# Two-layer attention, time-mix and expert kernel: projections ahead of turns, late weights and the attention's first inputs moved into the projection phase, and the shared groups of the experts reordered

## The chip, the cores and the metric

The kernel runs on one core of a Trainium2 chip. Its time is the device time of one execution, in microseconds (us). TensorE (PE) multiplies, VectorE (DVE) and ScalarE (ACT) work on rows, GpSimd (POOL) does small arithmetic and issues the indirect transfers, and SyncE (SP) issues nearly all other transfers.

## The reference

Input x is 2 sequences of 2048 tokens, 256 wide (4096 tokens). Two layers follow, each a parallel block: both halves read the same layer norm.

```python
xn = _layernorm(x)
x = x + attention(xn, w_qkv, w_out) + binarized_ffn(xn, w1, b1, w2, b2)
xn = _layernorm(x)
x = x + time_mix(xn, ...) + experts(xn, router, gate, up, down, shared_...)
```

- Attention: 16 heads of 16, rotary tables on q and k, causal softmax over 2048 tokens, projection by w_out.
- Binarized FFN: hidden 1024; each weight matrix is sign(w) times the mean of |w| of its row; gelu.
- Time-mix: x and the token before are blended by time_mix_k, _v and _r; k, v, r are their projections; a stable recurrence (running maximum p, numerator q) runs over the tokens, its result times sigmoid(r) is projected by W_o.
- Experts: softmax over 8 experts, the best 2 kept; silu(x gate) * (x up), then down (width 128); a shared expert of width 256 runs on every token.

## The kernel before, in words

The program is a row of phases. Within a phase every engine has its own program, and they meet on semaphores; between phases all engines meet.

**Projection phase** (`qkv_phase`). The 4096 tokens are 8 groups of 512 (G = 8). For each group: layer-norm statistics on DVE (`scales`, L280 to L290), the root on POOL (`ln.root`, L299 to L316), the normalized rows on ACT (`scaled`, L322), 8 transposes on PE (`ln.turn`, L332), a high part (ACT, L341) and a low part (DVE `low`, L346), and products of three float16 pairs on PE (`heads` for q and k, `values` for v, L102). DVE applies the rotary tables (`products` L741, `rotated` L749 and L750) and takes the low parts (`last`, L755). The stages are software-pipelined: `step(at)` gets the groups that stand at each stage, `rolling` runs the steps, the first and last written out, the middle ones in a hardware loop of two steps (`Fori`). `w.vector` and `w.tensor` (L133 to L180) find one power-of-two scale for w_qkv: the maximum over partitions goes through PE (L153, L155), then DVE writes the scaled high and low parts. SP loads x, weights and rotary tables, stores normalized parts (L662), q and k (L670) and v (L673); in its second step it also issues the loads of the weights that later phases use (`late_weights.load`, L393 to L400).

**Attention phase** (`attention_phase`). 8 iterations, each of one sequence and one group of heads. Softmax needs the row maxima before it; they are computed by entries that run ahead of the exponentials: an entry multiplies k by q on PE (L1253), adds the mask (L1259), and DVE reduces it (L1187); a "turn" entry transposes the maxima (L1245, L1174, L1177) and SP sends them into extra rows of q (`send_m`, L1083). `HEAD` entries run before the first exponential (L1216) of iteration 0, the others between its steps. Before them come the phase's own loads of ident, mask, k and q (L1059, L1045, L1052), and PE and ACT turn the late weights (L425, L438) in 12 groups: 4 ahead of the first entry, 8 between entries.

**Time-mix phase** (`rwkv_phase`). 8 groups of 512 tokens pass five stages; x of a group is loaded by L1776. The router's logits need the normalized parts of all 8 groups (`load_parts`, L1781). DVE then chooses experts and slots (L1871 to L1929), after which POOL scatters the rows to their experts by 64 indirect transfers (L1838). At its start SP clears the semaphores of the first two phases (`retired`).

**Expert phase** (`moe_phase`). `FIRST` shared groups run first, then 46 tiles of 128 rows of one expert each (about 2.6 us a tile), then the other shared groups. `shared(n)` is gate and up (L102 on PE, L2448 on ACT, L2349 and L2354 on DVE), `shared_out(n)` is down (PE) and L2381 (DVE). POOL gathers the experts' results back (64 transfers, L2288), the last 24 after the last tile, and DVE adds them (`finish`, L2406 and L2411).

## Time and profile before

| | |
|---|---|
| three timed runs | 1685.28 us (median), 1674.21, 1686.58 |
| profiled execution | 1673.15 us, span in the trace 1671.4 us |
| busy: PE, DVE, ACT, POOL | 78%, 76%, 59%, 19% of the span |
| mean granted TensorE clock | 0.907 of full speed |
| projections | 0 to 146 us |
| attention, 8 iterations | 146 to about 1012 us |
| time-mix, scatter included | 1231 to 1448 us |
| experts | 1448 us to the end |

The rows further down are of three kinds. A timeline row gives start, duration, engine, source line, operation, output and inputs, count, and in brackets the idle time ahead of it on that engine with what ended it. A DMA row on SPq gives the time that the issuing of its transfers took. A window row gives the busy time of each engine in a stretch, and the granted clock.

### The profile page before, as it was taken

How to read it: one execution, taken by the hardware profiler on the slowest of the kernel's cores; microseconds unless marked ns; L12 is line 12 of the kernel's file. 1: busy time of each engine (PE TensorE's matmuls, PEld its weight loads, DVE VectorE, ACT ScalarE, POOL GpSimd, SP SyncE). 2: the span in 40 equal slices, each digit the busy share in tenths (PEclk: the TensorE clock that was granted, in tenths of full speed). 3: DMA queues.
4: the chain of work that ended last, by engine and by line, in shares of the span. 5: the costliest groups of instructions: out<-in, count | busy, mean ns of one | idle time of the engine just before them, and what ended most of it. 6: DMA issues, size and time to landing. Idle time of an engine off the chain costs nothing. (4 is left out here: it accounts for less than half of the span.)

```text
span 1671.4 us, 27976 instructions
## 1 busy us (share of the span) xinstructions
PE 1300.7 (78%) x9558; PEld 589.5 (35%) x9558; DVE 1271.8 (76%) x1880; ACT 986.5 (59%) x1291; POOL 321.7 (19%) x574
## 2 busy tenths in 40 slices
PE   2783887888888888798888985988736866579987
PEld 1442322222222222222222211666513333258754
DVE  3994788988779788898888922578666999475677
ACT  2442355777768677787787895556335656246642
POOL 2210000110101101011100201322100057500563
PEclk9886589999899999999999998999957897789999
DMA  6787202140321303223031024556543044676865
GB/s 184 250 266 181 52 8 41 20 91 6 74 41 29 83 5 74 41 37 76 6 76 37 12 40 130 159 192 202 173 141 127 25 136 152 201 239 201 251 197 201
DMA packets 159863, 186.27 MB, mean 111 GB/s; under 512 B 19572, under 2 KB 135796, under 8 KB 158708
## 3 DMA queue, kind: packets, MB, share of 16 engines
q1 hardware_dynamic: 153304, 167.65, 35.7%
q0 software_dynamic: 6144, 16.79, 3.1%
q8 instruction: 73, 1.20, 0.3%
q14 instruction: 54, 0.44, 0.1%
q10 hardware_dynamic: 288, 0.20, 0.1%
HBM read 100.94 MB, written 83.36 MB: 110 GB/s over the span
## 5 line engine op out<-in xcount | busy, mean ns | idle before, releaser
L1216 ACT ACTIVATE att_prob<-att_score,late_score_scale 128x1024 f32<-128x1024 f32 (+3 forms) x640 | 594.5, 988 | 214.2 <-PE att_score L1318 212.4
L1187 DVE TENSOR_REDUCE att_m_part<-att_mx 128x2 f32<-128x1024 f32 (+3 forms) x408 | 473.4, 1160 | 98.8 <-PE att_mx L1259 50.4
L1302 PE MATMUL att_pv<-att_prob,att_v 128*32 128x512 f32 (+3 forms) x2560 | 316.4, 568 | 0.5 <-POOL att_prob L1151 0.2
L1318 PE MATMUL att_score<-att_qop,att_kop 50*128 50x512 f16 (+3 forms) x1280 | 257.3, 364 | 9.0 <-ACT att_prob L1216 5.9
L1253 PE MATMUL att_mx<-att_kop,att_qop 48*128 48x512 f16 (+3 forms) x944 | 177.4, 361 | 106.3 <-DVE att_m_part L1187 101.6
L1151 POOL TENSOR_SCALAR_AFFINE_SELECT att_prob<-att_prob 128x256 f32<-128x256 f32 x256 | 102.9, 406 | 762.2 <-ACT att_prob L1216 762.0
L1187 DVE TENSOR_REDUCE att_m_part<-att_mx_one 128x1 f32<-128x384 f32 (+1 forms) x336 | 221.1, 658 | 32.8 <-PE att_mx_one L1253 27.0
L1318 PEld LDWEIGHTS att_score<-att_qop,att_kop 50*128 50x128 f16 x1280 | 69.4, 95 | 281.4 <-ACT att_prob L1216 192.7
L1253 PE MATMUL att_mx_one<-att_kop,att_qop 48*128 48x384 f16 (+1 forms) x336 | 132.4, 394 | 20.3 <-DVE att_m_part L1187 16.7
L2066 PE MATMUL rwkv_prod<-rwkv_xm,late_mixT 128*128 128x512 f32 x192 | 101.2, 682 | 36.9 <-ACT rwkv_kvr L2029 25.1
L1253 PEld LDWEIGHTS att_mx<-att_kop,att_qop 48*128 48x128 f16 x944 | 50.8, 96 | 174.7 <-DVE att_m_part L1187 158.1
L1838 POOL DMA_INDIRECT rows<-rwkv_xs,routing_slot_i x64 | 67.2, 1050 | 141.6 <-DVE routing_slot_i L1929 111.4
L2288 POOL DMA_INDIRECT moe_yg<-results,routing_slot_i x64 | 66.0, 1032 | 128.7 <-DMA results<-moe_y 109.9
L1598 ACT ACTIVATE ffn_gelu<-ffn_hid_ps,late_b,late_a 128x512 f32<-128x512 f32 x64 | 49.2, 778 | 66.9 <-PE ffn_hid_ps L1639 51.3
L1546 DVE SCALAR_TENSOR_TENSOR ffn_hid<-ffn_gelu,late_hid_scale_scale,ffn_hid 128x512 f16<-128x512 f32 x64 | 52.0, 847 | 44.8 <-ACT ffn_hid L1606 44.8
L1302 PEld LDWEIGHTS att_pv<-att_prob,att_v 128*32 128x32 f32 x2560 | 51.4, 110 | 70.9 <-issue 46.4
L2066 PEld LDWEIGHTS rwkv_prod<-rwkv_xm,late_mixT 128*128 128x128 f32 x192 | 41.2, 221 | 89.2 <-issue 76.0
L1639 PE MATMUL ffn_hid_ps<-ffn_xp,late_w1T 128*128 128x512 f16 x256 | 63.7, 386 | 4.7 <-ACT ffn_gelu L1598 4.1
L1657 PE MATMUL ffn_out_ps<-late_w2T,ffn_hid 128*128 128x256 f16 x512 | 63.6, 279 | 0.0
L1253 PEld LDWEIGHTS att_mx_one<-att_kop,att_qop 48*128 48x128 f16 x336 | 32.1, 96 | 82.6 <-DVE att_m_part L1187 71.0
L2012 ACT ACTIVATE rwkv_xm<-rwkv_x,late_unmix 128x512 f32<-128x512 f32 x48 | 30.2, 710 | 51.3 <-DMA rwkv_x<-xn1T 51.3
L1657 PEld LDWEIGHTS ffn_out_ps<-late_w2T,ffn_hid 128*128 128x128 f16 x512 | 51.6, 101 | 11.5 <-issue 0.8
(259 smaller groups left out, 1921.6 us busy)
## 6 DMA issues: line engine op xcount, KB each, us to landing
moe_xt<-rows SPq DMA_DIRECT2D x46, 256.0 KB, 3.5
results<-moe_y SPq DMA_DIRECT2D x46, 256.0 KB, 2.8
qk<-qkv_parts SPq DMA_DIRECT2D x32, 256.0 KB, 3.8
va<-qkv_v SPq DMA_DIRECT2D x8, 1024.0 KB, 6.4
att_v<-va SPq DMA_DIRECT2D x8, 1024.0 KB, 5.2
rows<-att_zeros SPq DMA_DIRECT2D x8, 864.0 KB, 6.2
att_kop<-qk SPq DMA_DIRECT2D x48, 128.0 KB, 4.9
att_qop<-qk SPq DMA_DIRECT2D x186, 32.0 KB, 3.1
```

Source lines behind the costliest of these rows:

```text
L1151: nc.gpsimd.affine_select(out=at, in_=at, compare_op=ALU.is_ge, fill=0.0, base=0, pattern=[[0, 2], [1, P]], channel_multiplier=-1)\
L1187: nc.vector.tensor_reduce(cells[:, sides[0]:sides[-1] + 1, some], bank.rearrange("p a (h w) -> p a h w", w=w), AX.X, ALU.max).then_inc(m_f ...
L1216: nc.scalar.activation(prob[:, r % (PROBS * HP), :, n0:], score[:, r % 2, :, n0:], ACT.Exp, scale=late_weights.score_scale[:, 0:1])\
L1253: op = nc.tensor.matmul(bank[a][:, n * w:(n + 1) * w], qop[rows, slot, t, hp, i * P:(i + 1) * P], kop[rows, slot, hp, c * GT:c * GT + w], ...
L1302: op = nc.tensor.matmul(pv[at, n0:], v[:, slot, j, at], prob[:, (st * HP + h // 2) % (PROBS * HP), h % 2, n0:], start=(j == 0), stop=(j == ...
L1318: op = nc.tensor.matmul(score[:, r % 2, hh, n0:], kop[rows, slot, hp, j * P:(j + 1) * P], qop[rows, slot, t, hp, n0:], start=True, stop=True)
L1546: nc.vector.scalar_tensor_tensor(hid[:, slot, 1, m], gelu[:, m % GELUS], hid_scale.scale[:, 0:1], hid[:, slot, 0, m], ALU.mult, ALU.subtra ...
L1639: op = nc.tensor.matmul(hid_ps[:, m % 2], w1T[:, k, m * P:(m + 1) * P], xp[:, slot, part, k], start=(k == 0 and part == 0), stop=(k == KC ...
L1657: op = nc.tensor.matmul(out_ps[:, j], hid[:, slot, part, m, at], w2T[:, m], start=(m == 0 and part == 0), stop=(m == FC - 1 and part == 1))
L1838: nc.gpsimd.indirect_dma_start(rows_d[part], bass.IndirectOffsetOnAxis(slot_i[:, k, j:j + 1], 0), xs[:, c % XP, i], None)\
L2066: op = nc.tensor.matmul(prod[:, (n * NO + o) % PRODS], wT[:, w, k, c * P:(c + 1) * P], xm[:, b, w, k], start=(k == 0), stop=(k == KC - 1))
L2288: nc.gpsimd.indirect_dma_start(yg[:, at, k], None, results_d[part], bass.IndirectOffsetOnAxis(slot_i[:, k, j:j + 1], 0))\
```

## The change

1. **Projections.** The loops are written out (`unrolled` in place of `rolling`). On PE the weight scale's product stands ahead of the first turn, and in each step `heads` stands ahead of `turn`. The layer-norm statistics get two buffers. Of DVE's work `low` of the new group stands after the rotation of the one before. From the third group on, each step turns one of the 12 groups of late weights, the other 6 follow the last step; their banks are two halves of the bank of v. The late weights' loads are issued one SP step later, with the mask and the lift rows of the attention.
2. **The attention's inputs.** k and the first quarter of q of iteration 0 are loaded after the stores of group 6, ahead of those of group 7; the other three quarters and v after the last step. `HEAD` ends 3 entries after the first turn entry, where it was the second turn entry; the maxima's sends stand ahead of the second iteration's loads.
3. **Time-mix.** x of groups 2 and 3 is loaded ahead of the parts of groups 2 to 7; parts of groups 0 and 1 are loaded again behind these, for the experts. The clearing of semaphores moves to the end of SP's program.
4. **Experts.** `FIRST` goes from 2 to 3. Groups 0 and 1 read the parts left by the time-mix phase. Down weights, expert weights and shared groups are interleaved anew; after the tiles `shared(FIRST)` stands ahead of the last `tile_out`.

```diff
@@ SP, projections
-                if at[1] and not at[2]:
+                if at[2] and not at[3]:
                     late_weights.load(nc, sp, *late_ds)
+                    att_in.load_constants(sp, mask_d, lift_d)
                 if at[2]:
                     store_xn(*at[2])
                 if at[3]:
                     store_heads(*at[3])
-
-            rolling(sp, step, 4)
+                    if at[3][0] == G - 2:
+                        sp.wait_ge(qk_stored[0], 16 * QK * KC * (1 + G // 2))
+                        att_in.load_k(sp, qk_d, 0, 0, 0)
+                        att_in.load_q(sp, qk_d, 0, 0, 0, 0, att_in.first_in[0])
+
+            unrolled(step, 4)
+            for t in range(1, att_in.QB):
+                att_in.load_q(sp, qk_d, 0, 0, 0, t, att_in.second_in if t == 1 else att_in.rest_in[0])
@@ DVE, projections
+                for p in range(QK):
+                    if mid:
+                        products(*mid, p)
+                        rotated(*mid, p)
                 if new:
                     low(*new)
-                if mid:
-                    products(*mid, 0)
-                    rotated(*mid, 0)
-                    products(*mid, 1)
-                    rotated(*mid, 1)
@@ PE, projections
             def step(at):
                 new, mid = at
+                if new and not mid:
+                    w.tensor(nc, pe, qk_ps[0:1, 0, 0, 0:P], qk_ps[:, 0, 0, P:P + 1], ident[:, :], ones[:, :])
+                if mid:
+                    ...
+                    heads(*mid, 0)
+                    if mid[0] >= late_from:
+                        late(mid[0])
+                    heads(*mid, 1)
                 if new:
                     ln.turn(nc, pe, new[0], new[1], ident[:, :])
@@ attention
-    HEAD = ahead.index(("turn", 1)) + 1
+    HEAD = ahead.index(("turn", 0)) + 3
@@ SP, attention
-                load(0, 1, 1)
                 for t in range(LATE - 1):
                     send_m(0, 0, t, False)
+                load(0, 1, 1)
@@ SP, time-mix
-            for signal in retired:
-                sp.sem_clear(signal)
             load_x(0)
             load_x(1)
...
                 if m == B:
-                    for g in range(XP, G):
+                    load_x(B)
+                    load_x(B + 1)
+                    for g in range(XP, G + XP):
                         load_parts(g)
...
             groups(step, 5)
+            for signal in retired:
+                sp.sem_clear(signal)
@@ experts
-    FIRST = 2
+    FIRST = 3
@@ DVE, experts
             shared(0)
-            down_weights(slice(SHARED, SHARED + E))
-            for e in range(E):
+            for e in range(E // 2):
                 weights(e)
             shared(1)
             shared_out(0)
             owners()
+            for e in range(E // 2, E):
+                weights(e)
+            shared(2)
             shared_out(1)
+            dve.wait_ge(down_high, 2)
+            down_weights(slice(SHARED, SHARED + E))
+            shared_out(2)
             tile_x(0)
@@ PE, experts
+            shared(FIRST)
             tile_out(NTILES - 1, before)
-            shared(FIRST)
```

How the instructions stand at three places, before and after. In the start of PE's program, `qkv_qk_ps` is the bank of the products and of the weight scale's transpose, `qkv_turned` that of the turns. Before:

```order
L332 MATMUL qkv_turned<-qkv_ident,qkv_ln_xn 128x128 x8
L153 MATMUL qkv_qk_ps<-qkv_ident,qkv_w_qkv_top 1x128
L155 MATMUL qkv_qk_ps<-qkv_w_qkv_apart,qkv_ones 128x1
L590 UNCONDITIONAL_BRANCH
L590 ISA
L328 REGISTER_ALU
L332 MATMUL qkv_turned<-qkv_ident,qkv_ln_xn 128x128 x8
L833 ISA
L102 MATMUL qkv_qk_ps<-qkv_ln_hi,qkv_w_qkv_hi 128x512
```

After, the same engine from its start:

```order
L153 MATMUL qkv_qk_ps<-early_ident,qkv_w_qkv_top 1x128
L155 MATMUL qkv_qk_ps<-qkv_w_qkv_apart,qkv_ones 128x1
L338 MATMUL qkv_turned<-early_ident,qkv_ln_xn 128x128 x8
L102 MATMUL qkv_qk_ps<-qkv_ln_hi,qkv_w_qkv_hi 128x512
L102 MATMUL qkv_qk_ps<-qkv_ln_hi,qkv_w_qkv_lo 128x512
```

The scale's two products have moved ahead of the first turn, and the first group's products ahead of the second turn. The next place is SP at the end of the projections and the start of the attention. Before:

```order
L670 DMA qk<-qkv_parts 16x16x512 x4
L673 DMA va<-qkv_v 128x4x512
L670 DMA qk<-qkv_parts 16x16x512 x4
L673 DMA va<-qkv_v 128x4x512
L603 UNCONDITIONAL_BRANCH
L1056 UNCONDITIONAL_BRANCH
L1059 DMA att_ident<-in_ident 128x128
L1059 DMA att_mask<-in_mask 128x320
L1045 DMA att_kop<-qk 16x2x2048 x6
L1052 DMA att_qop<-qk 16x2x512 x18
L1064 DMA att_kop<-in_lift 2x8192 x2
L1073 DMA att_v<-va 128x2048
```

After, with the attention's buffers named `early_`:

```order
L744 DMA qk<-qkv_parts 16x16x512 x4
L747 DMA va<-qkv_v 128x4x512
L642 DMA early_kop<-qk 16x2x2048 x6
L649 DMA early_qop<-qk 16x2x512 x6
L744 DMA qk<-qkv_parts 16x16x512 x4
L747 DMA va<-qkv_v 128x4x512
L649 DMA early_qop<-qk 16x2x512 x18
L654 DMA early_v<-va 128x2048
```

Twelve loads stand between the last two groups' stores, and 19 more come ahead of the phase's end. The third place is PE after the last tiles of the experts; `moe_tile_p` is a tile's hidden, `moe_hid_p` a shared group's. Before, the last two tiles' down products and the first shared group behind them:

```order
L102 MATMUL moe_out_ps<-moe_down_p,moe_tile_p 128x256
L102 ISA
L102 MATMUL moe_out_ps<-moe_down_p,moe_tile_p 128x256 x5
L102 ISA
L102 MATMUL moe_out_ps<-moe_down_p,moe_tile_p 128x256
L102 ISA
L102 MATMUL moe_out_ps<-moe_down_p,moe_tile_p 128x256 x5
L102 MATMUL moe_gate_ps<-moe_xp,experts_shared_p 128x512 x6
L102 MATMUL moe_up_ps<-moe_xp,experts_shared_p 128x512 x6
```

After, from the last but one tile's down products:

```order
L102 MATMUL moe_out_ps<-moe_down_p,moe_tile_p 128x256 x5
L102 MATMUL moe_gate_ps<-routing_xp,experts_shared_p 128x512 x6
L102 MATMUL moe_up_ps<-routing_xp,experts_shared_p 128x512 x6
L102 MATMUL moe_gate_ps<-routing_xp,experts_shared_p 128x512 x6
L102 MATMUL moe_up_ps<-routing_xp,experts_shared_p 128x512 x6
L102 ISA
L102 MATMUL moe_out_ps<-moe_down_p,moe_tile_p 128x256
L102 ISA
L102 MATMUL moe_out_ps<-moe_down_p,moe_tile_p 128x256 x5
```

One shared group's gate and up now stand between the last two tiles' down products.

## Rows read from the trace of the kernel before

**Rows 1.** Busy us of PE, PEld, DVE, ACT, POOL, then the clock, by stretch.

```profile
39.60:137.70 98.10, 74.11 (x420) 45.19 (x418) 93.45 (x136) 43.91 (x76) 18.81 (x75) 0.88 0.75 241
156.20:189.30 33.10, 24.95 (x173) 13.06 (x173) 24.83 (x32) 4.69 (x8) 0.00 (x0) 0.50 0.55 124
189.30:200.00 10.70, 9.06 (x40) 1.75 (x39) 8.80 (x12) 5.80 (x8) 2.44 (x6) 0.50 0.01 3
323.00:426.00 103.00, 86.03 (x777) 25.72 (x772) 86.07 (x107) 76.15 (x86) 13.25 (x33) 0.97 0.23 47
```

**Rows 2.** Timelines of DVE and PE, the first 40 us.

```profile
7.56 1.75 DVE L174 TENSOR_REDUCE qkv_w_qkv_top<-qkv_w_qkv_w 128x1 f32<-128x1536 f32 x1
...
16.38 1.94 PE L332 MATMUL qkv_turned<-qkv_ident,qkv_ln_xn 128*128 128x128 f32 x8 [16.38 <-ACT qkv_ln_xn L322]
...
18.88 0.28 DVE L133 TENSOR_REDUCE qkv_w_qkv_top_all<-qkv_qk_ps 1x1 f32<-1x128 f32 x1 [9.56 <-PE qkv_qk_ps L153]
...
23.74 1.40 DVE L280 BATCH_NORM_STATS2 qkv_ln_stats<-qkv_xin 128x6 f32<-128x256 f32 x4
...
26.02 1.23 DVE L346 TENSOR_TENSOR qkv_ln_lo<-qkv_turned,qkv_ln_hi 128x1024 f16<-128x1024 f32 x1
...
39.63 1.23 DVE L741 TENSOR_TENSOR qkv_by_cos<-qkv_qk_ps,qkv_cos 128x1024 f32<-128x1024 f32 x1 [1.97 <-PE qkv_qk_ps L102]
```

**Rows 3.** Timeline of SP, the late weights' loads, first and last.

```profile
4.25 0.43 SPq L393 DMA_DIRECT2D staging_raw<-in_L_attn_W_k  x1
...
17.31 1.79 SPq L400 DMA_DIRECT2D late_first<-in_L_attn_time_first  x1
```

**Rows 4.** Timelines of DVE and SP, last stores to first maximum.

```profile
135.25 2.42 DVE L755 TENSOR_TENSOR qkv_parts<-qkv_rot,qkv_parts 128x1024 f16<-128x1024 f32 x2
...
136.56 2.57 SPq L670 DMA_DIRECT2D qk<-qkv_parts  x4
...
147.15 2.66 SPq L1045 DMA_DIRECT2D att_kop<-qk  x6
...
149.86 8.56 SPq L1052 DMA_DIRECT2D att_qop<-qk  x18
...
157.03 0.69 DVE L1187 TENSOR_REDUCE att_m_part<-att_mx 128x4 f32<-128x512 f32 x1 [10.35 <-PE att_mx L1259]
```

**Rows 5.** DMA part of the page: KB each, median us to landing.

```profile
qk<-qkv_parts SPq DMA_DIRECT2D x32, 256.0 KB, 3.8
```

**Rows 6.** Timelines of SP, ACT, DVE and POOL, time-mix phase to the first scatter.

```profile
1231.24 0.19 POOL L1826 MEMSET experts_ones<- 20x128 f32 x1 [54.09 <-POOLq L1367]
...
1234.52 1.28 SPq L1776 DMA_DIRECT2D rwkv_x<-xn1T  x2
...
1285.27 3.79 ACT L2012 ACTIVATE rwkv_xm<-rwkv_x,late_unmix 128x512 f32<-128x512 f32 x6 [17.17 <-DMA rwkv_x<-xn1T]
...
1286.64 4.07 DVE L1936 SCALAR_TENSOR_TENSOR rwkv_xm<-rwkv_x,late_mix,rwkv_xm 128x512 f32<-128x512 f32 x6 [5.50 <-ACT rwkv_xm L2012]
...
1294.31 0.17 DVE L1944 COPY rwkv_p<-rwkv_p 128x2 f32<-128x2 f32 x1 [3.60 <-ACT rwkv_kvr L2029]
...
1343.17 1.45 POOL L1838 DMA_INDIRECT rows<-rwkv_xs,routing_slot_i  x1 [111.43 <-DVE routing_slot_i L1929]
```

**Rows 7.** Timeline of PE, expert phase: the first tile.

```profile
1482.40 0.88 PE L102 MATMUL moe_gate_ps<-moe_xh,moe_expert_p 128*128 128x256 f16 x6 [1.23 <-DVE moe_xh L2387]
```

**Rows 8.** Timelines of PE and POOL, behind the last tile.

```profile
1610.62 0.84 PE L102 MATMUL moe_out_ps<-moe_down_p,moe_tile_p 128*128 x6 [2.31 <-DVE moe_tile_p L2354]
...
1615.62 0.94 POOL L2288 DMA_INDIRECT moe_yg<-results,routing_slot_i  x1 [7.20 <-DMA results<-moe_y]
...
1649.26 1.08 POOL L2288 DMA_INDIRECT moe_yg<-results,routing_slot_i  x1 [0.30 <-issue]
...
1653.25 2.78 PE L102 MATMUL moe_out_ps<-moe_down_p,moe_hid_p 128*128 128x256 f16 x24
...
1661.43 5.30 PE L102 MATMUL moe_out_ps<-moe_down_p,moe_hid_p 128*128 128x256 f16 x24 [5.40 <-DVE moe_base L2381]
```

312 lines of the change are left out of this document (172 added, 140 removed).

## The prediction

> **What bounds the kernel now.** I read the busy time of each engine by stretch first, and from it which engine each stretch waits for; then the timelines around the five places that the change touches; then the stores' landing time. In the steady projections DVE is busy 93.45 of 98.10 us, PE 74.11 [rows 1]: DVE bounds, with 4.65 us of idle in eight groups. In a later iteration of the attention PE and DVE are both busy 86 of 103 us at a clock of 0.97, and neither loses much to one other engine [rows 1]. The places with real gaps are five: DVE's 9.56 us wait for the weight scale's product at the start [rows 2]; the 19.4 us from the end of the last rotation (135.25 + 2.42 = 137.67) to the first maximum at 157.03 [rows 4]; the 33.1 us of maxima before the first exponential, in which DVE is busy only 24.83 [rows 1]; ACT's 17.17 us wait for x in the time-mix phase [rows 6]; and the end, where PE waits 5.40 us for DVE ahead of its last products [rows 8]. The change goes to all five. What it leaves alone is the bulk: iterations 1 to 7 of the attention, the FFN, the scatter, the 46 tiles.
>
> **Term A, the start of the projections.** The maximum of the weights is reduced by 7.56 + 1.75 = 9.3, but its product stands behind a turn that starts at 16.38, and so DVE gets it at 18.88; from there to the next group's statistics at 23.74 are 4.9 us of scale and split [rows 2]. With the product first, 9.3 + 0.6 + 4.9 gives 14.8, so the weights are no longer last. The turn stays where it was (it waits for ACT), ends at 18.3, and the high part (ACT, about 1) and the low part (1.23 for the second group's at 26.02 [rows 2]) follow: the first group's heads can start at 20.8, no longer behind the second turn. The first of them took 4.6 us at half clock; the rotation starts at 25.4, where it started at 39.63 [rows 2]: 14.2 us earlier, less 1.23 for the second group's low part, which now follows the first rotation: 13.0. What is late next is x of the fourth group. SP spends 17.31 + 1.79 - 4.25 = 14.9 us on the late weights' loads [rows 3]. They now start at about 17.6, behind x and tables of the third group, and end at 32.5; with the store behind them x is issued at 34 and, landing in about 4 as the store's 3.8 [rows 5], is there at 38.3. DVE wants it at 36.2 and loses 2.1. **A = 10.9** (6 to 14).
>
> **Term B, the steady steps.** Between 0 and DVE's whole idle of 4.65 us [rows 1]. PE's work grows by a late turn a step; a turn of 8 blocks takes 1.94 at half clock [rows 2], one of 4 half that, and PE has 24 us to spare in eight groups, so it is hidden; if PE were to be late, six times 1.0 would be the price. The turn's later place on PE is covered by the second statistics buffer. I take **B = 1.5**, nearer to nothing, since most of the idle is spread over short gaps. DVE then ends at T = 137.7 - 12.4 = 125.3.
>
> **Term C, the change-over.** Before, 19.4 us. Now SP bounds it. The stores of group 6 end about 7 us ahead of T and land 3.8 later [rows 5]; then 12 loads: 2.66 for k and a third of 8.56 for q [rows 4], 5.5 together, to T + 2.1; the stores of group 7, 2.57 and 0.65 for v, which could have gone at T - 1, to T + 5.3; the 18 loads of q, 8.56, to T + 13.9, and v. The phase ends there, and as the inputs are in place the first maximum follows in about 1.5: T + 15.4 against T + 19.4. The last six late turns on PE and their copies on ACT (6 times 0.6) lie beside SP's 8.6 us. **C = 4** (0 to 8).
>
> **Term D, the first iteration.** Thirteen entries, some 17 us of DVE work, move from ahead of the first exponential to between its steps. Ahead of it DVE is busy 75%, in an iteration 84% [rows 1], which would give 17/0.75 - 17/0.84 = 2.4. The maxima of the first turn, however, are sent and land with fewer entries to cover them; I put 4 us of idle there. **D = -1.5** (-6 to 5).
>
> In the trace the clock is still 0.50 from 189.3 to 200, where PE is busy 9.06 of 10.7 us [rows 1]: 1.2 GHz, after 33 us with 24.95 busy. The Trainium skill (TensorE: Matmul & The Clock Gate, section What's actually happening) says that sustained activity releases the throttle soon; by it the denser start would bring 2.4 GHz back early. The row speaks against it.
>
> **Term E, time-mix.** SP's first load goes at 1234.52, though the phase had begun by 1231.24 [rows 6]: 3.3 us of clearing, on the path of x. Moved to the end, it lies beside the scatter. x of group 3 was issued behind 12 part loads; ACT waited for it 17.17 [rows 6]. DVE lost 5.50 and 3.60 to that [rows 6]; with x ahead of the parts these 9.1 go. What is late next: the logits, since the parts come a little later, and DVE's choice waits for ACT's exponential; I put 2 us there. The slots are then ready 10.4 earlier, and with them the scatter, which starts at 1343.17 [rows 6] and is POOL's own pace to the end of the phase. Four more part loads (7 us of SP) stand ahead of the rows that POOL scatters, and these are needed 60 us later. **E = 10.4** (6 to 13).
>
> **Term F, the experts.** The first tile starts at 1482.40 [rows 7]. A third shared group now stands ahead of it. Its price lies between nothing, since DVE and PE wait for loads there, and the 7.8 us that a group takes PE behind the tiles; two groups' inputs are in place from the start, which gives some back. I take the middle: 3.5 later. Behind the tiles PE does six groups from 1611.3 to 1656.0 (1653.25 + 2.78), 7.8 each with its down product, and one fewer now [rows 8]. But POOL's last 24 gathers run from 1615.62 to 1650.34, 34.7 us, and wait for the last tile's results [rows 8]. With a shared group's 5.2 us in the 2.31 us gap ahead of the last down product, they start 2.9 later and end at 1653.2 on the old scale; landing (3), the last adds (1.8), the last sum (1.3) and the store (3) give 1662, against 1671.4: 9.5. **F = 9.5 - 3.5 = 6** (0 to 9).
>
> The sum is 10.9 + 1.5 + 4 - 1.5 + 10.4 + 6 = 31.3. Against the profiled execution, 1673.15, that is 1641.9. The other runs were 1674.21, 1685.28 and 1686.58; the four have a mean of 1679.8, and nothing in the change touches what makes them differ. I predict 1679.8 - 31.3 = **1648.5**.
>
> **Rivals.** (1) **SP's queue takes the gain of the change-over.** For it: SP's 12 loads stand ahead of group 7's stores and wait for a landing; 14.9 us of late loads stand ahead of x. Against: the counts above leave room. If C falls to 0 and x lands 4 us later, the lead is 23.3: 1656.5.
> (2) **The gathers bound the end harder.** Should each gather take as long as the first scatter, 1.45 [rows 6], with 0.30 between two, 24 of them take 42 us in place of 34.7: F = -1.3, 1655.8. For it: DVE's sums are now packed into the gathers' stretch. Against: in the trace they overlap already, at a mean of 34.7 / 24 = 1.45 with the gaps [rows 8].
> The Trainium skill (SBUF — State Buffer, section Who interferes with whom) has a rule for it: VectorE's fast two-port operations lock GpSimd out while it writes descriptors. The trace shows only the uneven lengths.
> (3) **The clock comes back early.** The first iteration then takes what a later one takes: DVE's 24.83 us at 84% are 29.6 in place of 33.1, and some 1.5 more behind it: lead 36.3, 1643.5. This is the time by the skill's rule on the clock (TensorE: Matmul & The Clock Gate).
> (4) **Slower than before: the clock stays low.** At 0.50 PE was busy 85% of its time [rows 1], so PE bounds there. PE's 86.03 us of an iteration at 0.97 would be up to 86.03 x 0.97 / 0.50 = 167, 64 more than the 103 us that it takes [rows 1]. If the low clock lasts through half an iteration more than it did, the lead of 31.3 is gone: 1680 and more. Against: PE idles less around the change-over than before.
> (5) **It doesn't do what it says.** The eight written-out steps must be fetched as instructions; if that stalls engines, or DVE's bound in the steady steps was all that counted, only E stays: lead 10, 1670.
>
> **Chances.** My forecast, 1638 to 1658: 0.54. Rival 1: 0.15. Rival 2: 0.08. Rival 3: 0.10. Rival 5: 0.09. Rival 4: 0.04. The range reaches from rival 3 with the upper ends of A, C and E together (some 10 us more, and the 4 that the runs' spread adds), 1629, to just under rival 5, 1668. One per cent, 16.8 us, is about what a measurement of this kernel can tell from no change; of the 1685.28; faster therefore means below 1668.4: the first four cases, 0.87; same is rival 5, 0.09; slower is rival 4, 0.04.
>
> **What the new profile would show.** A: the weight scale's products at about 9.4 ahead of the turn, the first rotation at 25.4, an idle of DVE for x near 36. B: rotations 13.1 apart. C: first maximum near 141. D: the first iteration ends 15 earlier. E: SP's first load right at the phase's start, ACT's wait for x gone, the scatter 10 earlier relative to the phase's start. F: first tile 3.5 later relative to the phase, POOL's gathers as what the last sums wait for. I am wrong if the last rotation ends after 131, if the low clock lasts past 230, or if the gathers' mean exceeds 1.7.

## The result, and the profile after

The changed kernel takes **1663.24 us** (median of 14 runs, 1658.70 to 1669.62), the kernel before 1676.89 us (14 runs, 1672.70 to 1686.58). The ratio is 0.9908, interval 0.9892 to 0.9925: 15.4 us less, 0.9%. That is 14.7 us above the 1648.5 that was predicted and outside the forecast's own band (1638 to 1658); it is inside the wide range (1629 to 1668) only because that was drawn to reach nearly down to rival 5. By the bound of one per cent it is "no change", to which the prediction gave 0.09. Of the 31.3 us that it had added up, about half came.

The profiled execution took 1663.91 us, its span is 1662.0 (before 1671.4), the mean granted clock 0.899 (before 0.907). The spans differ by 9.4 us only. To see where it went, I cut both traces at the same eight events and read the stretches between them (the events: the end of the last rotation, the first maximum, ACT's copy of o that ends iteration 0, the copy that ends iteration 7, POOL's first memset of time-mix, the first scatter, POOL's first operation of the experts, the first tile):

| stretch, us | before | changed | gained | forecast |
|---|---|---|---|---|
| start to the end of the last rotation | 137.67 | 132.14 | 5.5 | A + B = 12.4 |
| change-over, to the first maximum | 19.4 | 17.3 | 2.1 | C = 4 |
| iteration 0 of the attention | 166.8 | 173.0 | -6.2 | D = -1.5 |
| iterations 1 to 7 | 688.0 | 697.0 | -9.0 | 0 |
| to the time-mix phase | 219.4 | 219.0 | 0.4 | 0 |
| time-mix, to the first scatter | 111.9 | 101.0 | 10.9 | E = 10.4 |
| scatter, to the experts | 104.7 | 103.4 | 1.3 | 0 |
| experts, to the first tile | 34.6 | 39.0 | -4.4 | F's start, -3.5 |
| first tile to the end | 189.0 | 180.2 | 8.8 | F's end, 9.5 |

The last five rows and C came as forecast, within 2 us each. What is missing is in the projections, in iteration 0, and in iterations 1 to 7, whose program the change leaves alone.

**The start.** DVE in the changed kernel, from the weight scale to the first statistics that wait for x (start and duration in us, in brackets the idle time ahead and its releaser):

```profile
10.06 0.28 DVE L133 TENSOR_REDUCE qkv_w_qkv_top_all<-qkv_qk_ps 1x1 f32<-1x128 f32 x1 [0.77 <-PE qkv_qk_ps L153]
...
26.40 1.23 DVE L823 TENSOR_TENSOR qkv_by_cos<-qkv_qk_ps,qkv_cos 128x1024 f32<-128x1024 f32 x1 [2.95 <-PE qkv_qk_ps L102]
...
40.09 1.41 DVE L286 BATCH_NORM_STATS2 qkv_ln_stats<-qkv_xin 128x6 f32<-128x256 f32 x4 [2.88 <-DMA qkv_xin<-in_L_attn_x]
...
50.85 2.35 DVE L837 TENSOR_TENSOR qkv_parts<-qkv_rot,qkv_parts 128x1024 f16<-128x1024 f32 x2
```

The wait for the weight scale's product, 9.56 us before [rows 2], is 0.77. The rotation starts at 26.40 (forecast 25.4), the wait for x is 2.88 us (forecast 2.1). The second rotation's last step stands at 50.85 and stood at 60.18: A is 9.3.

**The steady steps.** From there the lead shrinks. The same step of the eight groups starts at 34.86, 50.85, 64.90, 77.92, 91.97, 105.31, 119.35 and 129.72: from the second one on, steps of 14.05, 13.0, 14.05, 13.3, 14.0 and 10.4, where before they were 13.4, 13.3, 13.4, 13.35, 11.9 and 9.7. The view of waits, 39.6 to 132.1, PE and then DVE (waited for: us in total, times, longest), and the busy times of that stretch:

```profile
PE qkv_qk_ps L102 <- DVE qkv_ln_lo L352: 19.1, 6, 5.5
```

```profile
DVE qkv_by_cos L823 <- PE qkv_qk_ps L102: 5.9, 4, 3.2
DVE qkv_ln_stats L286 <- DMA qkv_xin<-in_L_attn_x: 2.9, 1, 2.9
```

```profile
39.60:132.10 92.50, 69.22 (x396) 41.58 (x394) 83.36 (x126) 46.79 (x76) 19.02 (x75) 0.89 0.81 257
```

PE's first product of a group waits six times for DVE's low part, and four times DVE then waits for PE. DVE's idle is 9.1 us, 4.65 before [rows 1]. On DVE the low part of the new group now stands behind the rotation of the group before, and PE's products of the new group (`heads`) need it. What such a wait does to PE is seen in three successive groups (PE, 65 to 93 us):

```profile
65.04 0.39 PE L102 MATMUL qkv_qk_ps<-qkv_ln_hi,qkv_w_qkv_hi 128*128 128x512 f16 x1 [1.92 <-DVE qkv_ln_lo L352]
...
78.06 0.61 PE L102 MATMUL qkv_qk_ps<-qkv_ln_hi,qkv_w_qkv_hi 128*128 128x512 f16 x1 [3.73 <-DVE qkv_ln_lo L352]
78.46 0.63 PE L102 MATMUL qkv_qk_ps<-qkv_ln_hi,qkv_w_qkv_lo 128*128 128x512 f16 x1
...
83.92 0.38 PE L102 MATMUL qkv_qk_ps<-qkv_ln_hi,qkv_w_qkv_hi 128*128 128x512 f16 x1
...
92.11 0.39 PE L102 MATMUL qkv_qk_ps<-qkv_ln_hi,qkv_w_qkv_hi 128*128 128x512 f16 x1 [1.94 <-DVE qkv_ln_lo L352]
```

After 1.92 us of idle a product takes 0.38 us, after 3.73 it takes 0.61 to 0.63, twelve times in a row: 2.4 and 1.2 GHz (their starts are 0.22 and 0.43 apart). A second trace of the same kernel (experiment 12 below) has the low clock after a shorter idle too, and there it lasts for eight products:

```profile
91.25 0.61 PE L102 MATMUL qkv_qk_ps<-qkv_ln_hi,qkv_w_qkv_hi 128*128 128x512 f16 x1 [2.38 <-DVE qkv_ln_lo L352]
```

Behind slow products DVE can have to wait. After PE's 3.73 us wait it does, and the whole step is 1.05 us longer; two steps on, after a wait of 4.05 us, DVE waits 3.23:

```profile
83.50 1.22 DVE L823 TENSOR_TENSOR qkv_by_cos<-qkv_qk_ps,qkv_cos 128x1024 f32<-128x1024 f32 x1 [0.98 <-PE qkv_qk_ps L102]
...
110.88 1.23 DVE L823 TENSOR_TENSOR qkv_by_cos<-qkv_qk_ps,qkv_cos 128x1024 f32<-128x1024 f32 x1 [3.23 <-PE qkv_qk_ps L102]
```

**The change-over.** SP, and then DVE:

```profile
126.95 3.04 SPq L642 DMA_DIRECT2D early_kop<-qk  x6
130.03 2.75 SPq L649 DMA_DIRECT2D early_qop<-qk  x6
132.89 2.55 SPq L744 DMA_DIRECT2D qk<-qkv_parts  x4
...
136.16 10.60 SPq L649 DMA_DIRECT2D early_qop<-qk  x18
146.87 0.36 SPq L654 DMA_DIRECT2D early_v<-va  x1
```

```profile
149.43 0.69 DVE L1241 TENSOR_REDUCE att_m_part<-att_mx 128x4 f32<-128x512 f32 x1 [0.77 <-DVE att_neg_m L1217]
```

SP's queue is the path, as forecast. Its 18 loads of q started 4.0 us after the last rotation (1.3 sooner than forecast), but took 10.60 us where they had taken 8.56 [rows 4], and the first maximum came 2.7 behind their end, where 1.5 had been put: together the 1.9 between 15.4 and 17.3. In the second trace of this kernel (experiment 12) the change-over is 16.3.

**Iteration 0.** Stretches of the changed kernel: length, busy us of PE, PEld, DVE, ACT, POOL, then the clock:

```profile
149.40:167.00 17.60, 7.66 (x69) 3.53 (x68) 11.27 (x15) 0.00 (x0) 0.00 (x0) 0.50 0.09 36
167.00:200.00 33.00, 23.93 (x133) 6.08 (x131) 27.73 (x34) 10.45 (x12) 3.26 (x8) 0.55 0.27 41
200.00:230.00 30.00, 25.21 (x187) 7.11 (x187) 25.22 (x32) 16.53 (x20) 3.22 (x8) 0.78 0.16 50
230.00:240.00 10.00, 9.47 (x38) 1.58 (x34) 6.58 (x8) 4.77 (x5) 0.00 (x0) 0.50 0.06 14
```

The first exponential comes 17.6 us after the first maximum (33.0 before), and the rest of the iteration is 21.6 longer. Ahead of it PE waits for the maxima to come back:

```profile
166.32 0.61 PE L1359 MATMUL att_score<-early_qop,early_kop 50*128 50x512 f16 x2 [3.51 <-DMA early_qop<-att_m_row]
```

The clock comes up sooner than before, and from 230 to 240 it is down again at 1.2 GHz, where PE is busy 9.47 us of 10. The prediction had named a low clock past 230, and a last rotation after 131 (it ends at 132.14), as signs against it. The granted clock by ten microseconds, from 160 us on, in four kernels (two of them are experiments below, numbered as there):

| us | 160 | 170 | 180 | 190 | 200 | 210 | 220 | 230 | 240 | 250 |
|---|---|---|---|---|---|---|---|---|---|---|
| before | 0.50 | 0.50 | 0.50 | 0.50 | 0.50 | 0.70 | 0.83 | 0.99 | 0.84 | 1.00 |
| changed | 0.50 | 0.50 | 0.50 | 0.67 | 0.66 | 0.83 | 0.86 | 0.50 | 0.79 | 0.90 |
| changed, again (12) | 0.50 | 0.50 | 0.50 | 0.84 | 0.50 | 0.79 | 0.89 | 0.77 | 1.00 | 0.83 |
| old length of the head (2) | 0.50 | 0.50 | 0.50 | 0.50 | 0.75 | 0.83 | 0.95 | 0.88 | 1.00 | 0.83 |

**Time-mix and experts.** SP, DVE and POOL in the time-mix phase:

```profile
1238.43 1.28 SPq L1815 DMA_DIRECT2D rwkv_x<-xn1T  x2
...
1248.52 4.51 SPq L1815 DMA_DIRECT2D rwkv_x<-xn1T  x2
...
1259.69 25.46 SPq L1821 DMA_DIRECT2D routing_xp<-parts  x16
```

```profile
1290.58 0.17 DVE L1986 COPY rwkv_p<-rwkv_p 128x2 f32<-128x2 f32 x1 [1.00 <-ACT rwkv_kvr L2071]
```

```profile
1339.43 1.45 POOL L1880 DMA_INDIRECT rows<-rwkv_xs,routing_slot_i  x1 [100.67 <-DVE routing_slot_i L1971]
```

SP's first load goes at the phase's first instant (1238.43; POOL's memset is at 1238.43), ACT's 17.17 us wait for x is gone, and DVE's 5.50 and 3.60 [rows 6] have become one wait of 1.00. The end (PE and POOL):

```profile
1613.65 0.82 PE L102 MATMUL moe_out_ps<-moe_down_p,moe_tile_p 128*128 x6
...
1652.94 4.37 PE L102 MATMUL moe_out_ps<-moe_down_p,moe_hid_p 128*128 128x256 f16 x24 [2.17 <-DVE moe_base L2423]
```

```profile
1617.91 0.94 POOL L2330 DMA_INDIRECT moe_yg<-results,routing_slot_i  x1 [8.92 <-DMA results<-moe_y]
...
1649.73 1.05 POOL L2330 DMA_INDIRECT moe_yg<-results,routing_slot_i  x1 [0.30 <-issue]
```

The last tile's product comes 3.0 later than before, PE's last products 8.5 earlier. The 24 gathers take 32.87 us, 1.37 each with the gap; before 34.7, 1.45 each.

### The profile page after: what moved, and what is told of

It is laid out like the page before. It is cut to its first block and busy times, and to the rows that moved or that the text cites. A ratio compares the mean times of both kernels' runs of the same rounds, so it can differ in the third digit from the quotient of the medians.

```text
span 1662.0 us, 27637 instructions
## 1 busy us (share of the span) xinstructions
PE 1316.7 (79%) x9558; PEld 588.4 (35%) x9558; DVE 1271.5 (77%) x1880; ACT 987.9 (59%) x1292; POOL 319.4 (19%) x574
## 5 line engine op out<-in xcount | busy, mean ns | idle before, releaser
L1343 PE MATMUL att_pv<-att_prob,early_v 128*32 128x512 f32 (+3 forms) x2560 | 324.5, 581 | 0.5 <-POOL att_prob L1206 0.2
L1302 PE MATMUL att_mx<-early_kop,early_qop 48*128 48x512 f16 (+3 forms) x944 | 181.1, 367 | 118.0 <-DVE att_m_part L1241 106.2
L1359 PE MATMUL att_score<-early_qop,early_kop 50*128 50x512 f16 (+3 forms) x1280 | 261.0, 369 | 12.4 <-ACT att_prob L1270 5.9
L1359 PEld LDWEIGHTS att_score<-early_qop,early_kop 50*128 50x128 f16 x1280 | 69.5, 95 | 293.5 <-ACT att_prob L1270 188.7
L1302 PE MATMUL att_mx_one<-early_kop,early_qop 48*128 48x384 f16 (+1 forms) x336 | 134.1, 399 | 19.7 <-DVE att_m_part L1241 15.9
L1302 PEld LDWEIGHTS att_mx<-early_kop,early_qop 48*128 48x128 f16 x944 | 51.7, 97 | 190.9 <-DVE att_m_part L1241 165.9
L1343 PEld LDWEIGHTS att_pv<-att_prob,early_v 128*32 128x32 f32 x2560 | 51.8, 111 | 71.8 <-issue 50.2
L1302 PEld LDWEIGHTS att_mx_one<-early_kop,early_qop 48*128 48x128 f16 x336 | 32.2, 96 | 80.6 <-DVE att_m_part L1241 69.6
L1308 PE MATMUL att_mx<-early_mask 64*128 64x64 f16 x864 | 51.2, 201 | 0.0
```

The lines of the kernel that those rows point to most:

```text
L1302: op = nc.tensor.matmul(bank[a][:, n * w:(n + 1) * w], qop[rows, slot, t, hp, i * P:(i + 1) * P], kop[rows, slot, hp, c * GT:c * GT + w], ...
L1343: op = nc.tensor.matmul(pv[at, n0:], v[:, slot, j, at], prob[:, (st * HP + h // 2) % (PROBS * HP), h % 2, n0:], start=(j == 0), stop=(j == ...
L1359: op = nc.tensor.matmul(score[:, r % 2, hh, n0:], kop[rows, slot, hp, j * P:(j + 1) * P], qop[rows, slot, t, hp, n0:], start=True, stop=True)
```

## The experiments

All were timed beside the kernel before. The first eight shared one chip, in two groups of four (kernel before: 1680.16 us, 22 runs, and 1681.32, 24 runs); the last four two others. A stage is judged by its stretch in the one trace of each run, the whole by the ratio to the kernel before, with its 95% interval in brackets. The stretches are those of the table.

One yardstick first. Experiments 2, 6, 7 and 12 leave the projections of the changed kernel as they are, and their last rotation ends at 130.6, 132.5, 130.1 and 132.1 us. With the 132.14 of the table, the same code ends anywhere in 2.4 us; a shift of that size in one trace shows nothing.

**1. The low part between the two rotations.** This is the remedy that suggests itself: PE would get the low part half a rotation earlier.

```diff
 # DVE, projections
                 if mid:
                     products(*mid, 0)
                     rotated(*mid, 0)
+                if new:
+                    low(*new)
+                if mid:
                     products(*mid, 1)
                     rotated(*mid, 1)
-                if new:
-                    low(*new)
```

> The changed kernel, but in the projections DVE's low part of the new group stands between the two rotations of the group before it, not behind both. Theory: in the changed kernel PE's heads wait for that low part (1.92 and 3.73 us of idle ahead of heads at 65.04 and 78.06), fall back to 1.2 GHz in the wait, and DVE then waits for them (0.98 and 3.23 us); so steps of 13.5 us go to 13.1 to 13.2, and the last rotation ends at about 128.5 in place of 132.1. Rival: the late turns on PE make the steps long; then the end stays within 1 us of 132.1. In the time: 3 us less by the theory, nothing by the rival.

Measured: 1680.93 us (10 runs), ratio 1.0016, interval 0.9993 to 1.0040; the last rotation ends at 145.96, steps of 15.3 us. DVE, two steps:

```profile
66.57 1.23 DVE L352 TENSOR_TENSOR qkv_ln_lo<-qkv_turned,qkv_ln_hi 128x1024 f16<-128x1024 f32 x1 [5.39 <-ACT qkv_ln_hi L347]
...
81.87 1.23 DVE L352 TENSOR_TENSOR qkv_ln_lo<-qkv_turned,qkv_ln_hi 128x1024 f16<-128x1024 f32 x1 [2.12 <-ACT qkv_ln_hi L347]
```

The remedy failed. The turn stands behind both `heads` on PE, its high part behind the first rotation's cast on ACT; the low part can't be had earlier, and now DVE waits for it with the second rotation behind. So the low part's late place is bound to the turn's late place: heads and turn on PE, high part on ACT, low part on DVE, and heads on PE again are one ring, and moving one link moves the wait.

**2. The old length of the attention's head.**

```diff
-    HEAD = ahead.index(("turn", 0)) + 3
+    HEAD = ahead.index(("turn", 1)) + 1
```

> The changed kernel with the attention's HEAD as before (it ends at the second turn entry, not 3 entries after the first). Theory: the short head costs what iteration 0 lost: the lead over before falls from 7.6 us at the first maximum to 1.4 at the end of iteration 0, since 13 entries run between steps while PE waits for the sent maxima and stays at 1.2 GHz. With the old head the first exponential comes at about 180 (31 us after the first maximum), and iteration 0 ends at 317 in place of 322.4: 5 us less. Rival 1: iteration 0 is bound by PE at 1.2 GHz whatever the head; its end moves by under 1 us. Rival 2, my term D for the bare move: the old head makes it 1 to 2 us longer.

Measured: 1659.75 us (4 runs), ratio 0.9882 (0.9828 to 0.9936). Iteration 0 takes 165.7 in place of 173.0, with the first exponential at 179.03; experiment 12 will show that the short head, too, can take 167.6. The time is no different from the changed kernel's within the intervals.

**3. The late turns all behind the steps.**

```diff
-        late_from, late_each = 2, 1
+        late_from, late_each = G, 1
...
-                if mid and mid[0] == late_from - 1:
+                if mid and mid[0] == 1:
                     late_weights.signs(nc, act)
```

> The changed kernel with all 12 groups of late weights turned behind the last projection step, none within the steps. By the theory that the place of the low part makes the steps long, their length stays near 13.5 us (last rotation at 131 to 132). By the rival, late turns in the steps, the last rotation ends at 128 to 129. Behind it PE turns 12 groups, about 0.9 us each with ACT's copies, 11 us, beside SP's 10.6 us of loads: the first maximum stays about 17.3 us behind the last rotation, at most 1 more.

Measured: 1664.33 us (7 runs), ratio 0.9932 (0.9892 to 0.9972). The last rotation ends at 130.85, within what the same projections do by themselves; the change-over is 17.9, 0.6 longer. PE still waits six times for the low part, 21.3 us in sum. The late turns inside the steps are not what makes it wait, and no price of theirs is seen.

**4. The late loads at their old place.**

```diff
 # SP, projections
-                if at[2] and not at[3]:
+                if at[1] and not at[2]:
                     late_weights.load(nc, sp, *late_ds)
```

> The changed kernel with the late weights' loads issued one step earlier, where they stood before (from 4.3 us, ahead of x of the third group), mask and lift with them. Theory: SP is idle from 4.2 to 16.7 in the changed kernel, so the loads fit there nearly whole; x of the third group comes 3 us later but DVE waits there for PE anyway (2.95 us ahead of the first rotation); x of the fourth group comes early enough, and the 2.88 us wait at 40.09 goes. The last rotation ends 2.9 us earlier, 129.3. Rival: the 14.9 us of loads delay x of the third group past what the 2.95 us cover, or their traffic delays x and the weights at the start; then the gain is 0 to 1 us.

Measured: 1666.51 us (10 runs), ratio 0.9918 (0.9893 to 0.9944). The 2.88 us wait is gone, and another has come, for the group before:

```profile
26.20 1.40 DVE L286 BATCH_NORM_STATS2 qkv_ln_stats<-qkv_xin 128x6 f32<-128x256 f32 x4 [5.02 <-DMA qkv_xin<-in_L_attn_x]
```

The last rotation ends at 130.37, again within the spread, and the ratio shows nothing. The late loads keep SP for 13 to 16 us and delay one x or the other.

**5. The time-mix part alone**, on the kernel before: x of groups 2 and 3 ahead of the part loads, the semaphores cleared at the end.

```diff
 # SP, time-mix
-            for signal in retired:
-                sp.sem_clear(signal)
             load_x(0)
...
-                if m >= B and at[0] is not None:
+                if m > B + 1 and at[0] is not None:
                     load_x(at[0])
                 if m == B:
+                    load_x(B)
+                    load_x(B + 1)
                     for g in range(XP, G):
                         load_parts(g)
...
+            for signal in retired:
+                sp.sem_clear(signal)
```

> The kernel before with two edits of the time-mix phase alone: x of groups 2 and 3 loaded ahead of the parts of groups 2 to 7, and the clearing of semaphores moved to the end of SP's program. Theory: term E stands by itself; the time from the phase's start to the first scatter goes from 111.9 to 101.0 us as it did in the changed kernel, and the whole is 11 us shorter than before (ratio 0.9935). Rival: the gain is given back in the scatter, which waits for rows whose loads now come later; then the start of the experts moves by under 6 us. It also shows the attention's seven later iterations once more for a kernel whose attention is untouched: 688 us if the first trace of before was typical, about 700 if it was lucky.

Measured: 1672.11 us (10 runs), ratio 0.9948 (0.9911 to 0.9986), 8.7 us less (0.9935 and 11 were expected; the interval holds that). Time-mix takes 101.1 us where it took 111.9: all of term E. And a second thing: iterations 1 to 7, whose code is that of the kernel before, take 697.5 us in this trace. In the profile of before they took 688.0. The projections (137.54) and iteration 0 (167.0) are as before.

**6. Two shared groups ahead of the tiles**, the interleaving kept (DVE's `shared(2)` and `shared_out(2)` go behind the tiles with their loads).

```diff
-    FIRST = 3
+    FIRST = 2
...
-            shared(2)
...
-            shared_out(2)
```

> The changed kernel with two shared groups ahead of the tiles as before (their new interleaving and the inputs left in place stay), six behind, one of them still ahead of the last tile's down product. Theory, term F: the first tile comes 5 us earlier than in the changed kernel (about 34 us after the expert phase's start in place of 39.0), and the stretch behind the tiles, from the last tile's down product to the end, grows from 48.4 to 54 or more since DVE has one group of 5.3 us more; in sum 1 us more to 1 less. Rival: the gathers set the end anyway, so the tail stays at 48 to 49 and the kernel gets 4 to 5 us shorter than the changed one.

Measured: 1661.28 us (4 runs), ratio 0.9898 (0.9824 to 0.9971). The first tile comes after 30.6 us (changed 39.0, before 34.6), the rest takes 184.5 (180.2, 189.0): together 215.2, 219.2 and 223.6.

```profile
1476.76 1.46 PE L102 MATMUL moe_gate_ps<-moe_xh,moe_expert_p 128*128 128x256 f16 x6 [0.60 <-DVE moe_xh L2427]
...
1609.27 0.82 PE L102 MATMUL moe_out_ps<-moe_down_p,moe_tile_p 128*128 x6
```

So all of term F's 4.4 us, and more, comes from the rest of the change (the new interleaving, the inputs left in place, the end); the third group ahead of the tiles costs 8.4 and gives back 4.3. The 8.4 is clear; the other kernels with three groups ahead have 217.3 to 220.7 in sum on this chip, so the net loss is 2 to 5.5 us. Four runs can't show that in the time.

**7. The last tile's down product at its old place.**

```diff
 # PE, experts
-            shared(FIRST)
             tile_out(NTILES - 1, before)
+            shared(FIRST)
```

> The changed kernel with the last tile's down product ahead of the fourth shared group again, as before the change. Theory, term F: the last 24 gathers wait for that product's result; with it the gathers start some 3 us earlier, at about 9.5 us after the last but one tile's down product in place of 10.3 and more, and as they set the end, the kernel ends 2 to 3 us earlier. Rival: PE's 2.3 us wait ahead of that product comes back and every shared group behind it is that much later; DVE bounds the end, and the time is the same or 1 us longer.

Measured: 1663.33 us (10 runs), ratio 0.9905 (0.9876 to 0.9934). The gathers of the last tiles start at 1612.70 in a trace of 1658.4, 45.7 ahead of the end, where the changed kernel has 44.1; the rest from the first tile is 178.4, where the five other kernels on this chip with three groups ahead and the changed end have 178.4 to 181.6. No gain shown: both orders end alike.

**8. The turn between the two heads.** With the ring of experiment 1 in mind: PE does `heads(0)`, the turn, late turns, `heads(1)`; ACT casts the high part first; DVE's low part stands between the rotations.

```diff
 # PE, projections
                     heads(*mid, 0)
-                    if mid[0] >= late_from:
-                        late(mid[0])
-                    heads(*mid, 1)
                 if new:
                     ln.turn(nc, pe, new[0], new[1], ident[:, :])
                 if mid:
+                    if mid[0] >= late_from:
+                        late(mid[0])
+                    heads(*mid, 1)
                     values(*mid)
 # ACT, projections: high(*new) ahead of first_part(*mid, 0)
 # DVE, projections: low(*new) between the rotations, as in experiment 1
```

> The changed kernel with another order of a projection step: PE turns the new group between the two heads, ACT writes its high part before the first part of the rotation, DVE takes the low part between the two rotations. Moving the low part alone made each step 15.3 us, since DVE waited 2.1 us and more for a high part whose turn stood behind both heads. Theory: with the turn ahead of the second heads that wait is gone, PE starts its heads some 3 us before DVE needs them even at 1.2 GHz, and no step has DVE wait for heads: steps of 13.0, last rotation at 129 in place of 132.1. Rival: high part and turn are still too late for a low part between the rotations (DVE waits over 0.5 us a step), and the end is 132 or later.

Measured: 1663.26 us (10 runs), ratio 0.9921 (0.9890 to 0.9951). The same steps' starts:

```profile
66.39 2.42 DVE L837 TENSOR_TENSOR qkv_parts<-qkv_rot,qkv_parts 128x1024 f16<-128x1024 f32 x2
79.48 2.42 DVE L837 TENSOR_TENSOR qkv_parts<-qkv_rot,qkv_parts 128x1024 f16<-128x1024 f32 x2
92.57 2.42 DVE L837 TENSOR_TENSOR qkv_parts<-qkv_rot,qkv_parts 128x1024 f16<-128x1024 f32 x2
```

The steady steps are 13.1 us, what term B had counted on; DVE waits for no other engine between 66 and 100 us, and PE waits 1.01 for the low part and keeps 2.4 GHz. The first two steps are 16.0, the second since DVE waits 2.87 us for PE, so the last rotation ends at 129.51, only 0.6 to 2.9 ahead of the changed projections.

**9 and 10. The better pieces together.** The late loads are split: the small ones one SP step earlier, the large ones at the new place. Experiment 10 is experiment 8 with that split; experiment 9 has, besides, `HEAD` and `FIRST` at their old values (as in experiments 2 and 6).

```diff
 # SP, projections
+                if at[1] and not at[2]:
+                    late_weights.load_small(nc, sp, *late_ds)
                 if at[2] and not at[3]:
-                    late_weights.load(nc, sp, *late_ds)
+                    late_weights.load_large(nc, sp, *late_ds)
```

> The changed kernel with what the runs so far point to, together: the order of a projection step with the turn between the two heads; the late weights' small loads (biases, mixes, decay: 8 us of issuing) from 4.3 us on, in SP's idle time, and the large ones where the change put them; the attention's head as before the change; two shared groups ahead of the tiles. Theory: the prices measured one by one add up. Last rotation at 124 to 125 (the 2.88 us wait for x and the long second and third steps gone, steps of 13.1), iteration 0 as long as before (166 to 167 us from the first maximum), the expert phase 215 us in place of 219. Against the changed kernel 8 + 5 + 4 = 15 us less, median 1648, ratio to before 0.981. Rival: TensorE's clock eats the gain of the projections in iteration 0, as it did in others; then 9 less, 1654.

> The changed kernel with the projections' part alone of the combination: turn between the heads, low part between the rotations, the late weights' small loads early. Theory: last rotation ends at 124 to 125 in place of 132.1, first maximum at 142 in place of 149.4; iteration 0 stays at about 170 us from there; 7 us less than the changed kernel in the trace. Rival: SP's queue is what bounds (late copies, stores and loads in one queue), so steps of 16 us come back elsewhere, and the last rotation ends after 128.

Measured, on another chip on which the kernel before takes 1726.74 us (19 runs): experiment 9 1707.98 (8 runs), ratio 0.9901 (0.9870 to 0.9933); experiment 10 1711.19 (10 runs), ratio 0.9922 (0.9893 to 0.9951). The last rotation ends at 126.02 and 128.59, but iteration 0 takes 169.5 and 174.1. Neither ratio differs from the changed kernel's.

**11 and 12. All of it with the old end, beside the changed kernel itself.** Experiment 11 is 9 with 7's order; experiment 12 is the changed kernel, unaltered, on the same chip.

> The combination of e10 with the last tile's down product ahead of the next shared group again (e7's order). Beside it on the same chip stands the changed kernel once more, since the combination ran on a chip on which every kernel's expert phase took some 45 us more. Theory: the trace prices hold (last rotation 8 us earlier, iteration 0 some 4 shorter, expert phase 4 to 5 shorter), so this kernel is 13 to 17 us faster than the changed one on the same chip, about 0.8 to 1.0%. Rival: the gains ahead of the attention are taken back by TensorE's clock in iteration 0; then 5 to 8 us faster.

> The changed kernel unchanged. Theory: what differs between its first trace and that of before in the attention's iterations 1 to 7 (697.0 us against 688.0) was chance in the trace of before; they take 697 to 701 here too, and the time from the last rotation to the first maximum, in iteration 0 and in the phases behind repeats within 2 us: 17.3, 173, 101, 39.0. The ratio to before is 0.990 to 0.993. Rival: iteration 0 varies by itself by more than the 5 us that I put on the head; then it may be as short as 167 here.

Measured, on a third chip, kernel before 1722.01 us (17 runs): experiment 11 1704.10 (6 runs), ratio 0.9869 (0.9835 to 0.9904); the changed kernel 1711.40 (12 runs), ratio 0.9921 (0.9893 to 0.9949). The combination is 7.3 us faster than the changed kernel in the medians, about half of what was expected; the intervals of the two ratios overlap a little. By stretch the combination gains 3.4 us in the projections, 7.9 ahead of the first tile and 4.1 behind it, and loses 3.4 in iteration 0, 3.1 in the FFN's stretch and 1.0 in the scatter. The changed kernel's iteration 0 took 167.6 us here, with a clock of 0.60 and 0.88 behind the first exponential:

```profile
148.40:166.00 17.60, 7.66 (x69) 3.51 (x68) 11.27 (x15) 0.02 (x1) 0.00 (x0) 0.50 0.10 40
166.00:200.00 34.00, 24.50 (x154) 6.95 (x152) 29.26 (x36) 11.71 (x14) 3.27 (x8) 0.60 0.28 43
200.00:316.00 116.00, 95.39 (x775) 26.80 (x772) 96.52 (x121) 68.98 (x74) 10.94 (x27) 0.88 0.12 28
```

## Why the prediction was right in part, and wrong in one step

**A, the start: right, 9.3 us for 10.9.** Every event came as named and in order: product at 9.43, first rotation at 26.40 for 25.4, x as the next to be late. The first rotation came 1.0 later and the wait for x was 0.8 longer. Experiment 4 shows that the wait for x comes from the late loads in front of it: it moves to another x when they move.

**B, the steady steps: the step that failed.** I wrote that B lies "between 0 and DVE's whole idle" and that "the turn's later place on PE is covered by the second statistics buffer". The buffer covers the statistics; nobody had asked about the low part. It moved behind the rotation, and PE's next product needs it. I had named a price for a late PE, "six times 1.0", but for the late turns' work, and kept it out of the bounds. The low part had been priced once, at the start (1.23 us behind the first rotation), and not where it recurs every step. Measured: PE waits 19.1 us for it in six places, is at 1.2 GHz behind the 3.73 us wait, and DVE pays 5.9; B is 5.5 - 9.3 = **-3.8** for +1.5, and between -2.2 and -3.8 in the five traces with these projections. That the low part's ring is the cause is shown by experiments 1 and 8, in which the waits move with it: steps of 15.3 us, and of 13.1 with DVE waiting for no other engine. Experiment 3 shows that it isn't the late turns. What the term could have given over the whole stretch is not shown: even experiment 8 takes 1.7 us more than before from the second rotation to the last, because of its one step of 16.0. The Trainium skill (TensorE: Matmul & The Clock Gate, section What's actually happening) says that an idle TensorE is throttled. Here it was at the low clock after 3.73 us of idle, and in the second trace after 2.38, and not after 1.92 and 1.94.

**C, the change-over: mechanism right, size off by 1.9 us.** SP's queue sets it; the 18 loads were sized by the row of before, 8.56, and took 10.60, and the 1.5 from their end to the first maximum was 2.7. Over the traces of the changed kernel the change-over is 17.3 and 16.3.

**D, iteration 0: the sign was right, the size is not settled.** The forecast's mechanisms are all in the trace: the first exponential 15.4 us sooner after the first maximum, 3.51 us of wait for the sent maxima, the 13 entries' work between the later steps. The price was -6.2 in the first trace and -0.8 in the second of the same kernel (experiment 12), so most of the gap to -1.5 is what this stretch varies by. Over all traces the short head (the changed `HEAD`) gives 167.6 to 174.1 us (nine traces, mean 170.7), the long one (the old `HEAD`) 165.7 to 171.1 (five, mean 168.0): some 3 us for the long head, with ranges that overlap and kernels that differ in other places too. Rival 3, the clock back early, was half seen: it rises at 190 us, 20 sooner than before, and is down again at 230. The traces of before and of experiment 2 have no second fall; those of experiments 9 and 11, with the long head too, have one (0.53 and 0.50 at 230), so the head doesn't set it. What does stays open.

**E, time-mix: right, 10.9 for 10.4**, and shown alone by experiment 5 (10.8).

**F, the experts: right in sign and parts, 4.4 for 6.** The start cost 4.4 for 3.5, the end gave 8.8 for 9.5. But the source was put in the wrong place: I had taken the third group as the gain at the end and its price at the start as small (3.5, called the middle between 0 and 7.8, which is 3.9). Experiment 6 shows that it loses more at the start than it gives back; the rest of the change gives 8.4 without it. Rival 2 did not come: the gathers' mean is 1.37 us where it was 1.45 (and 1.40 in experiment 5, with the old end). The rule of the Trainium skill on who locks GpSimd out (SBUF — State Buffer, section Who interferes with whom) was not put to the test by this: DVE's sums did not get denser, it is busy 30.01 of the 32.87 us of gathers, and was 31.85 of 34.72.

**What I had not put in the sum: iterations 1 to 7.** "Nothing in the change touches what makes them differ" was said of the runs; of the trace I took for granted that 688.0 us was the stretch's time. Experiment 5, with the attention of before, took 697.5; the changed kernel 697.0 here and 700.6 on the third chip; the other ten kernels 700.2 to 704.0. What differs is TensorE's clock. These are the seven iterations before, in experiment 5, in the changed kernel and in experiment 6 (busy us of PE, PEld, DVE, ACT and POOL, then the clock):

```profile
323.82:1011.86 688.04, 586.09 (x5174) 170.61 (x5172) 552.33 (x679) 525.29 (x585) 88.77 (x221) 0.97 0.22 45
324.52:1022.05 697.53, 596.19 (x5174) 172.57 (x5172) 552.70 (x679) 525.21 (x585) 88.76 (x221) 0.95 0.22 45
322.43:1019.41 696.98, 594.74 (x5174) 172.06 (x5172) 552.39 (x679) 525.23 (x585) 88.94 (x221) 0.96 0.22 45
318.93:1022.90 703.97, 602.80 (x5174) 173.54 (x5172) 553.13 (x679) 524.90 (x585) 88.76 (x221) 0.94 0.22 44
```

The instructions are equal in number and DVE's and ACT's work is equal within a microsecond; PE's busy time goes up by 16.7 us as the granted clock goes down, and the stretch with it, by 15.9. So part of the missing 9.0 is a short draw in the one profile of before. Part may be real: the two traces of the old attention, 688.0 and 697.5, are both below eleven of the twelve of the new one. Without this row the table's gain is 18.4 us, while the medians say 13.7 and the ratio 15.4, which leaves room for a loss of 3 to 5 us here. Two traces of the old attention can't settle it, and why the clock should be lower stays open. The base, too, was a bit high: 1679.8 for a median of 1676.9.

So of the 31.3, beside that row: B missed by 5.3, D by 4.7 (mostly spread), C by 1.9, A and F by 1.6 each, and the FFN, E and the scatter gave 2.2 more. Rival 1 came half true, since SP's queue took 1.9 of C's 4 and x landed 0.8 later than counted, but no rival held the loss in B. Rival 5's stalls in the written-out steps are not seen: of DVE's 9.1 us of idle 5.9 are for PE and 2.9 for x. Rival 4, a low clock for half an iteration more, did not come at that size. The claimed chance of 0.87 for a gain over 1% leaned on bounds of which B's, with its low end at 0, was wrong. A step moved behind another can cost more than the idle that was there before. That the time still fell into the wide range is partly luck: the misses add up to 12.9 us beside the seven iterations, and the range had room for 19.5.

## What to carry to other kernels

When a step is moved on one engine, follow its output to the next engine and round the ring back to where it began, in the steady state and not only at the start: "covered by a buffer" holds for what the buffer holds alone. The loss then has two parts, the wait itself and the clock that it can take from TensorE afterwards; look at the durations behind each wait (here of 2.38 us and more). And before a stretch's time of a single profile is used as a base, or a shift in one is called a gain, take a second trace of the same code: here the same 7 iterations took 688.0 and 697.5 us, nearly as much apart as the largest term forecast, and the same projections end within a spread of 2.4 us.

## What the hardware showed beside that

- **Two clocks in one row of steps.** TensorE held 2.4 GHz after idle times of 1.92 and 1.94 us and was at 1.2 GHz after 3.73 us, in successive steps 14 us apart; in a second trace of the same kernel it was at 1.2 GHz after 2.38 us. The alternating steps of 13.0 and 14.05 us follow from it.
- **A busy TensorE at 1.2 GHz.** From 230 to 240 us it was busy 9.47 of 10 us at a granted clock of 0.50, after a stretch at 0.78. Six of the 14 traces have 0.50 in that window, the second trace of the same kernel has 0.77.
- **Chips differ by 45 us on one stage pair.** On the second and third chips the scatter takes some 8 us longer in the four kernels traced, and the experts' part from the first tile some 40 (the changed kernel in experiment 12: 110.9 and 223.2 us, where the table has 103.4 and 180.2). PE then stops amid the tiles for nothing that the profile names (experiment 9, PE):

```profile
1565.12 1.46 PE L102 MATMUL moe_out_ps<-moe_down_p,moe_tile_p 128*128 x6 [4.36 <-issue]
...
1576.81 1.46 PE L102 MATMUL moe_gate_ps<-moe_xh,moe_expert_p 128*128 128x256 f16 x6 [9.38 <-issue]
```

  The kernel before is slower there by as much (1722 to 1727 in place of 1677 to 1681 us), so the ratios can be compared; it has no trace on these chips, and the cause wasn't tried.
- **Indirect gathers at a near constant pace.** 24 gathers took 1.37 us each with their gap of 0.30, and 1.45 before, beside a DVE that was busy 91% and 92% of that time.
